# Two edge passes of a graph network: pairs of half-array products become four 64x64 tiles, with the halves of an edge block on the partition halves

## What is computed

```
h    = gelu(gelu(edge_inv @ W1) @ W2)            # once for keys (Wk), once for values (Wv)
out1 = concat([x_src, x_src[:, :, None] * edge_sh[:, None, :]])     # 64 + 64*8 columns
key  = out1 * (h_k @ Wk3);   value = out1 * (h_v @ Wv3)
scal = concat([q * key[:, :64], sum_s(q * key[:, d, s] * edge_sh[:, s])])
alpha = edge_weight * exp(scal @ W_logit - max) / segment_sum
out  = segment_sum(value * sqrt(alpha)) @ W_out
```

## Time and profile before

| | before |
|---|---|
| median of 3 runs (lowest to highest) | 4333.0 us (4331.6 to 4335.09) |
| span of the profiled execution | 4328.3 us |
| busy: PE, DVE, ACT, POOL | 77%, 87%, 50%, 43% |

### The profile page before, as it was taken

The page is one execution under the profiler, slowest core; times in us unless marked ns, Lnnn a source line. Parts: engine busy times, 40 slices in busy tenths (PEclk is TensorE's granted clock), DMA queues, the critical chain, the costliest instruction groups (busy, mean ns, idle before and its releaser), DMA issues. The chain is left out here.

```text
span 4328.3 us, 65784 instructions
## 1 busy us (share of the span) xinstructions
PE 3344.0 (77%) x20105; PEld 1485.8 (34%) x20105; DVE 3769.3 (87%) x6296; ACT 2147.9 (50%) x4398; POOL 1865.8 (43%) x3682
## 2 busy tenths in 40 slices
PE   5665555566499999999982999999999995177176
PEld 2111111212144444444431444444444442122122
DVE  8999999899788888888888888888888886898898
ACT  6999987576243434444432444444444442075076
POOL 0100555000577777777751666666666665000000
PEclk9989888677699999999995999999999997589589
DMA  4763999765255555555540333333333332545544
GB/s 162 303 261 146 330 354 359 237 203 184 84 143 151 142 140 143 150 143 142 142 113 17 92 92 92 93 92 94 92 92 93 93 93 66 209 178 193 185 169 179
DMA packets 373210, 675.88 MB, mean 156 GB/s; under 512 B 74685, under 2 KB 274941, under 8 KB 361217
## 3 DMA queue, kind: packets, MB, share of 16 engines
q1 hardware_dynamic: 297392, 559.11, 39.3%
q0 software_dynamic: 39568, 78.78, 6.7%
q10 hardware_dynamic: 35904, 33.79, 2.6%
HBM read 399.80 MB, written 271.65 MB: 155 GB/s over the span
## 5 line engine op out<-in xcount | busy, mean ns | idle before, releaser
L735 POOL DMA_INDIRECT arena<-h_table,srci x808 | 784.6, 971 | 302.1 <-issue 204.4
L830 PE MATMUL banks<-arena 128*128 128x500 bf16 x1440 | 421.3, 425 | 285.6 <-DVE arena L1482 229.9
L1773 DVE TENSOR_TENSOR arena<-banks,arena 128x1024 f32<-128x1024 f32 x404 | 493.7, 1222 | 63.3 <-PE banks L934 56.0
L1886 DVE TENSOR_TENSOR arena<-banks,arena 128x512 f32<-128x512 f32 x808 | 518.6, 684 | 32.3 <-PE banks L1037 8.7
L1894 DVE TENSOR_TENSOR arena<-banks,arena 128x512 f32<-128x512 f32 x808 | 517.0, 681 | 1.3 <-PE banks L1043 1.3
L1167 ACT ACTIVATE arena<-arena,h 128x128 bf16<-128x128 f16 x1440 | 454.6, 387 | 81.9 <-DVEq L1398 41.0
L1326 ACT ACTIVATE arena<-banks 64x256 f32<-64x256 f32 x808 | 305.2, 378 | 337.7 <-PE banks L1069 330.7
L1057 PE MATMUL banks<-arena 128*64 128x256 f32 x3232 | 438.5, 392 | 0.5 <-DVE arena L1896 0.5
L1043 PE MATMUL banks<-arena 64*128 64x512 f32 x1616 | 436.3, 618 | 0.9 <-DVE arena L1894 0.9
L940 PE MATMUL banks<-arena 128*64 128x256 f32 x3232 | 427.4, 385 | 0.0
L1470 DVE TENSOR_SCALAR arena<-arena,agg 128x500 bf16<-128x500 f16 x1440 | 416.5, 367 | 0.2 <-DVE h L1462 0.2
(11 more groups left out here) (302 smaller groups left out, 6387.2 us busy)
## 6 DMA issues: line engine op xcount, KB each, us to landing
arena<-c_flat SPq DMA_DIRECT2D x75, 1562.5 KB, 6.8
slots<-arena SPq DMA_DIRECT2D x90, 1000.0 KB, 4.3
arena<-hs_dump SPq DMA_DIRECT2D x404, 128.0 KB
arena<-mask_rows SPq DMA_DIRECT2D x50, 781.2 KB, 4.2
arena<-in_edge_attr SPq DMA_DIRECT2D x202, 128.0 KB
arena<-placed SPq DMA_DIRECT2D x202, 128.0 KB
xs_dump<-arena SPq DMA_DIRECT2D x202, 128.0 KB
hs_dump<-arena SPq DMA_DIRECT2D x202, 128.0 KB
```

Source lines behind the costliest of these rows:

```text
L735: pool.indirect_dma_start(out=xs[par][:, k * D:(k + 1) * D], out_offset=None, in_=h_table, in_offset=bass.IndirectOffsetOnAxis(ap=srci[:, ...
L830: last = pe.matmul(ps[4 + r % 2][:, 0:BW], row_hot[r][:, k * P:(k + 1) * P], col_hot[r][:, k * BW:(k + 1) * BW], start=k == 0, stop=k == K ...
L1773: V.tensor_tensor(bt_pair[i].rearrange("p (j n) -> p j n", j=2), banks[:, 5 * COLS:7 * COLS].rearrange("p (j n) -> p j n", j=2), h2k[t % 2 ...
L1886: V.tensor_tensor(dt_[j % 2], ps[3 + j % 2][:, :], xat[t % 3], ALU.mult).then_inc(dt_sb, 1)
```

## The change

Both passes now use 64 rows by 64 columns of the array for every product but the transpositions and the logits, four such tiles (row half by column half) at a time. Of a turn's 512 edges, one half lies on partitions 0 to 63 and the other on 64 to 127.

- Hidden layers, basis and value: 256 edges an instruction, four instructions where two of 512 edges (or two of 256 with 128 columns) stood.
- Keys, own parts and messages: 128 edges an instruction. The components are no longer paired on the two partition halves: eight products of 64 rows are added up in PSUM where four of 128 rows were.
- DVE's `p2_rows` and `p2_values` take 1024 columns an instruction: per turn rows, values, own, rows, values, where four rows, four values and one own stood. Both halves of a turn share two banks for the basis and two for the value product.
- ACT's copies `xat` (four) and `x0t` become one copy of 128x512, and the two gelus of the second hidden layer one.
- `p1_second` is done one turn earlier, after the transposition of the turn before; `p1_keys` no longer stands behind it.
- In the second pass the second half of a turn's messages is done in the next turn, after that turn's first value products; the pass has one turn of lag less.
- W_out is loaded (18 DMAs) between the passes instead of before the first; 11 loads fewer stand before the first pass.
- `hs_dump` holds a turn as two halves of 64x256; the buffers of the second hidden layer are three instead of two.

The core of the diff (the functions before are printed above):

```diff
+            def p1_keys(t, h):
+                pe.wait_ge(bt_sb, t * 2 + h + 1)
+                for n in range(4):
+                    s_ = 4 * h + n
+                    slot = (s_ % 2 * 2 + s_ % 4 // 2) * (TW // 2)
+                    for r, c in tiles:
...
-                    p1_turned(t - 1)
-                if edge(t):
-                    p1_second(t)
+                    p1_basis(t - 1, 0)
                 if edge(t - 2):
-                    kmm(t - 2, 2)
-                    kmm(t - 2, 3).then_inc(yk_ps, 1)
+                    p1_keys(t - 2, 1).then_inc(yk_ps, 1)
+                if group_done(t - 4):
+                    p1_fold(t, (t - 4) // 4)
                 if edge(t - 3):
                     p1_logits(t - 3)
-                pe.wait_ge(h1_sb, min(t + 2, T))
-                if group_done(t - 4):
-                    p1_fold((t - 4) // 4)
                 if edge(t):
                     p1_transpose(t)
+                if edge(t + 1):
+                    p1_second(t + 1)
                 if edge(t - 1):
-                    pe.wait_ge(bt_sb, t * 2 - 1)
-                    tb(t - 1, 2)
-                    tb(t - 1, 3).then_inc(tb_ps, 1)
-                    p1_half(t - 1)
+                    p1_basis(t - 1, 1)
+                    p1_own(t - 1)
+                    p1_keys(t - 1, 0).then_inc(half_k, 1)
...
+            def p2_basis(t, h):
+                at(dt_sb, t * 2 + h, pe)
+                for i in range(2):
+                    for q, r in tiles:
+                        last = pe.matmul(ps[q][rows_of(r), i * (TW // 2):(i + 1) * (TW // 2)], sel[rows_of(q), 2 * h + i, rows_of(q)],
+                                         sht2[t % 2][rows_of(q), r * (TW // 2):(r + 1) * (TW // 2)], start=True, stop=True)
+                last.then_inc(tv_ps, 1)
...
+            def p2_value(t, h):
+                at(vt_sb, t * 3 + h, pe)
+                for i in range(2):
+                    for q, r in tiles:
+                        last = pe.matmul(ps[2 + q][rows_of(r), i * (TW // 2):(i + 1) * (TW // 2)], v3[2 * h + i][rows_of(q), rows_of(q)],
+                                         hv[t % 2][rows_of(q), r * (TW // 2):(r + 1) * (TW // 2)], start=True, stop=True)
+                last.then_inc(y_ps, 1)
...
+                at(msgr_sb, t - 1, pe)
+                pe.wait_ge(xat_sb, t + 1)
+                for q, r in tiles:
+                    cols = r * (TW // 2) + q * P
+                    last = pe.matmul(ps[6 + q][rows_of(r), 0:P], v3[4][rows_of(q), 0:D], hv[t % 2][rows_of(q), cols:cols + P], start=True, stop=True)
+                last.then_inc(own_ps, 1)
...
+            def p2_message(h):
+                for n in range(4):
+                    s_ = 4 * h + n
+                    slot = (s_ % 2 * 2 + s_ % 4 // 2) * (TW // 2)
+                    for r, c in tiles:
+                        last = pe.matmul(ps[4 + r][rows_of(c), 0:P], wo[s_][rows_of(r), :], vt[h][rows_of(r), slot + c * P:slot + (c + 1) * P],
+                                         start=s_ == 0, stop=False)
...
                 pe.wait_ge(msg_sb, t + 1)
+                pe.wait_ge(vt_sb, min(t + 1, T - 1) * 3 + 2)
...
-            for t in range(-1, T + 2):
-                if 0 <= t - 1 < T:
-                    pe.wait_ge(hidden_in[(t - 1) % 2], ((t - 1) // 2 + 1) * 64)
-                    for j in (0, 1):
-                        p2_basis(t - 1, j)
-                    for j in (0, 1):
-                        p2_value(t - 1, j)
-                if 0 <= t - 2:
-                    pe.wait_ge(vt_sb, t * 5 - 5)
-                    p2_message(2)
-                    p2_message(3)
-                    p2_message(4).then_inc(msg_ps, 1)
-                if 0 <= t - 1 < T:
-                    for j in (2, 3):
-                        p2_basis(t - 1, j)
-                    for j in (2, 3):
-                        p2_value(t - 1, j)
+            pe.wait_ge(wo_in, 16 * 2 * (S + 1))
+            for t in range(-1, T + 1):
+                if 0 <= t < T:
+                    pe.wait_ge(hidden_in[t % 2], (t // 2 + 1) * 64)
+                    p2_basis(t, 0)
+                    p2_value(t, 0)
+                    p2_own(t)
+                if 0 <= t - 1:
+                    pe.wait_ge(vt_sb, t * 3)
+                    p2_message(1)
+                    p2_message_own().then_inc(msg_ps, 1)
+                if 0 <= t < T:
+                    p2_basis(t, 1)
+                    p2_value(t, 1)
                 if t + 1 < T:
                     p2_turned(t + 1)
-                if 0 <= t - 2:
-                    p2_back(t - 2)
-                if 0 <= t - 1 < T:
-                    at(msg_sb, t - 1, pe)
-                    pe.wait_ge(vt_sb, t * 5 - 3)
-                    p2_message(0)
-                    p2_message(1).then_inc(half_ps, 1)
-                    p2_own(t - 1)
+                if 0 <= t - 1:
+                    p2_back(t - 1)
+                if 0 <= t < T:
+                    at(msg_sb, t, pe)
+                    pe.wait_ge(vt_sb, t * 3 + 1)
+                    p2_message(0).then_inc(half_ps, 1)
...
+            def p2_rows(t, h):
+                dve.wait_ge(tv_ps, t * 2 + h + 1)
+                dve.wait_ge(xat_sb, t + 1)
+                at(vt_sb, t * 3 if h else t * 3 - 2, dve)
+                V.tensor_tensor(dt_[h].rearrange("p (s n) -> p s n", s=4), banks[:, 0:2 * COLS].rearrange("p (s n) -> p s n", s=4),
+                                xat[t % 3].rearrange("p (o n) -> p o n", o=1).to_broadcast([P, 4, TW // 2]), ALU.mult).then_inc(dt_sb, 1)
+            def p2_values(t, h):
+                dve.wait_ge(y_ps, t * 2 + h + 1)
+                dve.wait_ge(dt_sb, t * 2 + h + 1)
+                at(msg_ps if h else half_ps, t, dve)
+                V.tensor_tensor(vt[h], banks[:, 2 * COLS:4 * COLS], dt_[h], ALU.mult).then_inc(vt_sb, 1)
...
             for t in range(T):
-                for j in (0, 2):
-                    p2_rows(t, j)
-                    p2_rows(t, j + 1)
-                    p2_values(t, j)
-                    p2_values(t, j + 1)
-                p2_values(t, 4)
+                p2_rows(t, 0)
+                p2_values(t, 0)
+                p2_own(t)
+                p2_rows(t, 1)
+                p2_values(t, 1)
...
-                for half in range(2):
-                    for k in range(2):
-                        copied = act.activation(xat[r][half * D:(half + 1) * D, k * (TW // 2):(k + 1) * (TW // 2)],
-                                                ps[0][k * D:(k + 1) * D, 0:TW // 2], ACT.Copy)
-                copied.then_inc(xat_sb, 1)
-                at(vt_sb, t * 5 - 10, act)
-                act.activation(x0t[r], ps[0][:, TW // 2:TW], ACT.Copy).then_inc(xat_sb, 1)
+                at(vt_sb, t * 3 - 6, act)
+                act.activation(xt[r], ps[7][:, :], ACT.Copy).then_inc(xat_sb, 1)
```

More of the change, by code:

```diff
@@ L262, in build @@
         lgt = cw(P)
[L263 to L266, removed]
+        h2 = [cw(TW) for _ in range(3)]
+        h2k, h2v = [v[:, 0:TW // 2] for v in h2], [v[:, TW // 2:TW] for v in h2]
+        bt = [cw(2 * TW) for _ in range(2)]
         prod = [cw(TW) for _ in range(2)]
@@ L707, in _ @@
             pool.wait_ge(agg_ps, 4)
-            for v in (wb, wl, k3[4], wo[4], wo[5], sht[0], sht[1]):
+            for v in (wl, sht[0], sht[1]):
                 z = pool.memset(v, 0.0)
@@ L924, in _ @@
             pe.wait_ge(weights_in, 1)
[L925 to L941 removed]
+            tiles = [(q, r) for q in range(2) for r in range(2)]
@@ new lines, in p1_own, with p1_hidden @@
+            def p1_own(t):
+                at(prod_sb, t, pe)
+                pe.wait_ge(h2_sb, t + 1)
+                for r, c in tiles:
+                    pe.matmul(ps[6 + r][rows_of(c), P:2 * P], k3[S][rows_of(r), :], h2k[t % 3][rows_of(r), c * P:(c + 1) * P], start=True, stop=True)
+            def p1_hidden(t):
+                pe.wait_ge(ea_in[t % 2], (t // 2 + 1) * 16)
+                at(h2_sb, t, pe)
+                for r, c in tiles:
+                    last = pe.matmul(ps[r][rows_of(c), 0:TW // 2], w1[rows_of(r), rows_of(c)], eat[t % 2][rows_of(r), :], start=True, stop=True)
+                last.then_inc(h1_ps, 1)
@@ L961, in p1_logits @@
+                last.then_inc(h2_ps, 1)
             def p1_logits(t):
@@ L1335, in p2_back @@
                 at(run_sb, t, act)
-                act.activation(msgr, ps[7][:, 0:TW // 2], ACT.Copy).then_inc(msgr_sb, 1)
-            for t in range(-1, T + 2):
-                if 0 <= t - 2:
-                    p2_message(t - 2)
+                act.activation(msgr, ps[6][:, 0:TW // 2], ACT.Copy).then_inc(msgr_sb, 1)
+            for t in range(-1, T + 1):
+                if 0 <= t - 1:
+                    p2_message(t - 1)
                 if t + 1 < T:
                     p2_turned(t + 1, (t + 1) % 3)
-                if 0 <= t - 2:
-                    p2_back(t - 2)
+                if 0 <= t - 1:
+                    p2_back(t - 1)
```

241 lines of the change are left out of this document (105 added, 136 removed).

## The result

The changed kernel takes 4223.45 us (median of 4 runs, 4219.97 to 4226.87) against 4332.3 of the kernel before beside it (4326.21 to 4335.09): a ratio of 0.9751, 95% interval 0.9739 to 0.9763. The forecast was 4182. The gain is in the second pass, 104 us; the first pass, for which the forecast had 34 us, gained nothing.

The account below looks back on a forecast made before the run. PE was taken to set the second pass, POOL's fetches the first after the change: span 4328.3 - 117 (second pass) - 34 (first) = 4177, so 4182 as median. Range 4130 to 4265, the forecast's own 4150 to 4215.

Parts of the forecast that it names:

- forecast loop: Second pass: DVE and PE steps in sequence over shared banks make a turn of 5.72 us, 6.3 before; gain 117 us.
- `p2_values` 0 waits for its result (.05): Second-pass loop: DVE's `p2_values` 0 starts .05 us after `p2_rows` 0, each running 1.222.
- Rival 1: Both passes: rounds of 128 columns cost about .14 us, second-pass loop 6.02, time 4243; chance 20%.
- rival 5: PE in both passes: tiles run two at a time, turns 9.7 and 7.4 us, about 5400; chance 2%.
- Rival 4: PE in both passes: weight loads no longer hide, .05 us a round, time 4516; chance 6%.
- Rival 3: More gain: a shape change from 64x64 costs .10, POOL reaches its floor, loop 5.63, time 4148; chance 10%.
- Costs of nothing: W_out's 18 loads between passes (11 us of SP's queue, hidden), 11 fewer early loads, `hs_dump` halves, second gelu: 0 each.
- Of its .28 of waits I keep .1: First pass: of POOL's .28 us of waits a turn, .1 beside component stores stays; turn 5.2, gain 34 us.
- DVE needs some 4.85: First pass: after the change DVE needs some 4.85 us a turn, so POOL's 5.11 ends the turn.
- most of the .54 goes: First pass: most of DVE's .54 us a turn of waiting for PE goes, at `product` and the second basis.
- rival 2: The first pass gains nothing because POOL already sets it; time 4216; chance 12%.
- POOL reaches its floor: First pass: POOL's waits beyond its constant all go, turn 5.11 us, gain 50 us.

Follow-up runs that it names:

- e3: The changed kernel with the first half's messages in the second pass moved behind the next turn's first basis: 4169.4 us, ratio 0.9617 to 0.965.
- e4: The changed kernel with `p2_back(t - 1)` put behind `p2_message(0)`, two more shape changes a turn in the second pass: 4270.2 us, ratio 0.9849 to 0.9882.
- e6: The changed kernel with component stores spread and only fetches 0 and 2 of each four: 4113.9 us (one run), first pass 4.866 a turn.
- e1: The changed kernel with the six component stores of every sixteenth first-pass turn issued one a turn: 4193.5 us, ratio 0.9673 to 0.9706.
- e7: The changed kernel with a third buffer for fetched rows and POOL let a turn further ahead: 4176.6 us, ratio 0.9621 to 0.9667.
- e8: The changed kernel with spread component stores, third buffer, and first-half messages behind the next turn's first basis: 4124.4 us, ratio 0.9499 to 0.9529.
- e9: The changed kernel with first-half messages behind the next basis, plus four one-column memsets a turn on POOL in the second pass: 4177.9 us.
- e10: The changed kernel with first-half messages behind the next basis, plus four one-column copies a turn on ACT in the second pass: 4174.4 us.

## Why the prediction was right and wrong

**Second pass: the mechanism was right, the size off by .07 a turn.** The forecast loop was 5.72. Leg by leg on the timeline, with .05 from the first start of a product to its stream, as in the earlier trace rows (.06 for the transpositions, whose first two take .28 instead of .22): `p2_rows` 0 to the stream of the second value product, 2800.91 to 2803.51 + .05, 2.65 (forecast 2.604); products and shape to 2804.53 + .06, 1.03 (1.005); transpositions and shape to 2805.34 + .05, .80 (.805); `p2_message` 0 to 2806.26, .87 (.88); basis, drain and signal to 2806.70, .44 (.43). The step that failed most is "`p2_values` 0 waits for its result (.05)": the wait is .09 (2800.91 + 1.23 to 2802.23), and the two DVE instructions take 1.23, not 1.222. The rest are hundredths. With .52 a turn instead of .58 the pass gives 104 us, not 117; e3 and e4 show by removing from and adding to the loop that it is this loop.

**Rounds of four at the pace of pairs: right.** .215 and .11 were taken from the earlier trace rows and are measured. Rival 1 (.14 a round) and rival 5 (two tiles at a time) fall. Rival 4 (loads no longer hide) falls too: PEld is busy 300 of 400 us and the rounds keep their pace, so the loads stand beside the products. By the rule of the Trainium skill (TensorE: Matmul & The Clock Gate, Part 3: Packing small matmuls — row/col tiling) that loads overlap only products of other row groups they should not have, since two column tiles share each row half; the trace does not agree. That part of the Trainium skill also lets a load run ahead when it goes into a background weight buffer, which would fit; no run here tells the two apart. (Rival 4's sum has a slip: 32 x .05 is 1.6, not 1.7, and its time 4498.) Rival 3's cheaper change of shape falls with e4's .143.

**DVE: right.** Four instructions of 1024 columns at 1.21 to 1.23 and one of .41. The wait that the forecast put before the second value product is there: by starts, 2802.86 + .22 to 2803.51, .43.

**Costs of nothing: right.** The 18 loads of W_out take 11.3 us of SP's queue, from 2258; from the last `times` to the first basis of the second pass 101 us pass (2253.2 to 2354.3), 104.6 before.

**First pass: the failed step is "Of its .28 of waits I keep .1".** POOL kept all of them and more: 69 us, .34 a turn. The step before it came out in its number, "DVE needs some 4.85" is 4.866 in e6, but partly by luck: "most of the .54 goes" is not what happened, `times` waits as before, and DVE's shorter busy time made up for it. What was wrong is why POOL waits. I kept only those beside the burst of component stores and let the others go with a faster PE and DVE. But with the burst spread (e1) 44 us remain, some 14 of them the beat of 28 turns and the rest that store, and with a third buffer (e7) 7: POOL waits for the store of fetched rows because two buffers don't cover it, burst or not. The earlier trace rows already had 18 waits, 40.9 us (35 of the 45 beyond the constant), against that store, and the change leaves these stores, their queue and their buffers as they were. So rival 2, at 12%, is what happened in the first pass; its 4216 is 7 us from the result: 12.5 by which the second pass gave less than 117, less some 5 by which the stretch after it is shorter in the profile of the changed kernel. "POOL reaches its floor", the end of rival 3, is real, 5.07, but only once the waits are gone. The time lies in the stated range, 4130 to 4265, but not in the forecast's own, 4150 to 4215: the range held because it was wide enough for rival 2, not because the sum was right in both passes.

## What to carry to other kernels

A faster loop is worth nothing while another engine's chain sets the turn; before crediting a stage with a gain, ask for each wait of that other chain what ends it, and whether the change touches that. Waits that come in a beat (here every 16 turns) can point to a burst in a queue; one more buffer took away more of them (62 of 69 us) than spreading the burst did (25). In a loop over shared buffers, what counts is which work stands between the release and the reuse: reordering gave .32 us a turn at no less work.

## What the hardware showed that was not expected

- Four 64x64 tiles that share row and column halves keep a round every .11 us (128 fp32 columns) or .215 (256), with all their weight loads beside them.
- A change between 64x64 tiles and full 128x128 transpositions costs .143 us in the mean of one each way (e4), as it did for pairs of half arrays (.145).
- Twice the instructions (65784 to 129416) cost nothing while PE waited for DVE .43 a turn: no such stop is in the changed kernel's second pass. Where that slack was gone (e3, e8, e9, e10), PE stopped for its instructions .15 to .85 us at a time.
- A store of fetched rows issued behind six other stores and a load let its waiter go some 4.7 us after its issue; with two buffers such waits made the turn 5.39 where the fetches alone need 5.07.
